# The second attention's pooling branch: values copied and exponentials scaled by another engine, a bias folded once

## What is computed

```python
q = jnp.broadcast_to(slot_query, (Bx, NS, D))            # 16 slots
o = q + _mha(q, x, x, d_Wq, d_bq, d_Wk, d_bk, d_Wv, d_bv, d_Wo, d_bo)
# _mha: scores = (q Wq + bq)(x Wk + bk) / 4 ; attn = softmax(scores)
#       out = (attn (x Wv + bv)) Wo + bo
# then: 16 experts, one per slot, work on o; a last attention reads o from every token
```

## Time and profile before

| | |
|---|---|
| median of 3 runs | 1344.31 us (1343.42 to 1347.88) |
| profiled execution | 1347.85 us, span 1346.1 us |
| mean granted TensorE clock | 0.984 of 2.4 GHz |
| TensorE busy | 1280.9 us, 95% of the span |
| VectorE busy | 927.0 us, 69% |
| ScalarE busy | 805.5 us, 60% |
| POOL busy | 747.9 us, 56% |
| chain that ended last | TensorE 86%, VectorE 5%, DMA 3%, ScalarE 2% |

### The profile page before, as it was taken

How to read it: one execution, slowest core, us unless ns; L and a number is a source line. 1 busy time by engine, 2 the same in 40 slices (tenths; PEclk the granted TensorE clock), 3 DMA queues, 4 the chain that set the end, 5 groups by cost and what they waited for, 6 DMA issues and landing times.

```text
span 1346.1 us, 38344 instructions
## 1 busy us (share of the span) xinstructions
PE 1280.9 (95%) x14758; PEld 1143.9 (85%) x14758; DVE 927.0 (69%) x2426; ACT 805.5 (60%) x1794; POOL 747.9 (56%) x836
## 2 busy tenths in 40 slices
PE   7999999997999999999999988999999998899898
PEld 6888888886899999999999977899999997555476
DVE  3899999997576566555555027999999997221386
ACT  3676776663666777777676435666666665332453
POOL 1377777765478777777876034566666643100231
PEclk8999999998999999999999989999999999999999
DMA  5665554543667676777766811631111110599811
GB/s 173 214 223 192 189 168 165 190 166 108 231 214 217 223 223 220 226 232 228 218 220 224 327 44 29 236 116 49 49 49 56 56 32 29 215 430 429 322 64 64
DMA packets 103892, 237.52 MB, mean 176 GB/s; under 512 B 8992, under 2 KB 86176, under 8 KB 91296
## 3 DMA queue, kind: packets, MB, share of 16 engines
q1 hardware_dynamic: 97568, 218.29, 47.1%
q0 software_dynamic: 6144, 16.79, 3.9%
HBM read 174.22 MB, written 60.82 MB: 175 GB/s over the span
## 4 chain that ended last, share of the span: by engine, by line
PE 86%; DVE 5%; DMA 3%; ACT 2%; issue 2%; SPq 0%; POOL 0%; DVEq 0%; ACTq 0%; PEldq 0%; POOLq 0%
PE ps L1640 13%; PE psT L1625 6%; PE ps L648 6%; PE psS L625 5%; PE ps L802 5%; PE ps L852 5%; PE psT L634 4%; PE ps L661 4%; PE psS L1625 3%; PE ps L1625 3%; PE ps L785 2%; PE ps L815 2%; PE ps L742 2%; PE psT L640 2%; PE ps L1878 2%
## 5 line engine op out<-in xcount | busy, mean ns | idle before, releaser
L1593 POOL TENSOR_TENSOR wb_lo<-arena,wb_hi 128x2048 fp32r<-128x2048 f32 x64 | 298.0, 4657 | 96.7 <-ACT wb_hi L1713 96.7
L1640 PE MATMUL ps<-wb_hi,hT_hi 128*128 128x256 f32 x528 | 152.0, 288 | 2.5 <-DVE hT_lo L1766 2.5
L634 PE MATMUL psT<-arena 32*128 32x128 f32 x2048 | 151.2, 286 | 0.4 <-ACT arena L955 0.4
L1640 PE MATMUL ps<-wb_lo,hT_hi 128*128 128x256 f32 x528 | 149.3, 283 | 0.0
L1640 PE MATMUL ps<-wb_hi,hT_lo 128*128 128x256 f32 x528 | 148.4, 281 | 0.0
L625 PE MATMUL psS<-arena 32*128 32x256 f32 x1024 | 142.8, 397 | 1.2 <-ACT arena L955 0.5
L1713 ACT CAST wb_hi<-arena 128x1024 fp32r<-128x1024 f32 x128 | 130.6, 1045 | 11.3 <-DMA arena<-w_dram 10.7
L634 PEld LDWEIGHTS psT<-arena 32*128 32x128 f32 x2048 | 126.5, 189 | 1.1 <-issue 0.6
L1236 POOL TENSOR_TENSOR arena<-arena,eps_sb 128x1 f32<-128x1 f32 x96 | 23.8, 248 | 164.7 <-DVE arena L1113 114.2
L1778 DVE TENSOR_TENSOR arena<-ps,arena 128x512 f32<-128x512 f32 (+1 forms) x39 | 25.4, 650 | 117.4 <-PE ps L1640 77.0
L625 PEld LDWEIGHTS psS<-arena 32*128 32x128 f32 x1024 | 95.2, 191 | 9.9 <-issue 6.7
(11 more groups left out here) (400 smaller groups left out, 3920.5 us busy)
## 6 DMA issues: line engine op xcount, KB each, us to landing
arena<-wset_dram SPq DMA_DIRECT2D x24, 2048.0 KB, 14.5
xs_rows<-arena SPq DMA_DIRECT2D x33, 1024.0 KB, 5.0
arena<-w_dram SPq DMA_DIRECT2D x32, 1028.0 KB, 6.0
arena<-w_dram SPq DMA_DIRECT2D x32, 1024.0 KB, 5.9
arena<-w_dram SPq DMA_DIRECT2D x7, 2052.0 KB, 13.5
w_sb<-xs_rows SPq DMA_DIRECT2D x33, 256.0 KB, 2.7
xs_rows<-arena SPq DMA_DIRECT2D x33, 256.0 KB, 5.6
arena<-ctxT_dram SPq DMA_DIRECT2D x63, 128.0 KB, 2.3
```

The costliest lines, as they stand in the source:

```text
L634: nc.tensor.matmul(psT[:, b, j * P:(j + 1) * P], kbd[p, (k - 1) % 3, c, par, :], qT[p, (k - 1) % 3, c, :], start=j == 0, stop=False, skip_ ...
L1593: nc.gpsimd.tensor_tensor(wb_lo[:, u % 2, part], wb_raw[:, u % 2, part], wb_hi[:, u % 2, part], ALU.subtract).then_inc(w_g.sem, 1)
L1640: last = nc.tensor.matmul(ps[5][:, t * D:(t + 1) * D], hp[:, f, t * P:(t + 1) * P], wp[:, f, :], start=f == 0 and t == 0 and n == 0, stop= ...
```

## The change

The values' bias leaves the loop. Ahead of the steps TensorE multiplies `dbv` (now a column, spread over 128 columns as the stationary operand) with the output weights `do` into ps[4], and VectorE adds this to the row `dbo` before its first step; TensorE's step 0 waits for that. In the loop ScalarE copies the values without bias, one step later than VectorE did (for k-5, behind the copy L952 and ahead of the exponentials L955), and scales the exponentials by the reciprocals in two instructions, behind a wait for the reciprocals. VectorE loses the addition L1213, the product L1088 and the negation L1173: the queries and their bias are folded with a minus sign, so that L1170 takes a minimum, which is the negated maximum, and L1037 applies a scale of -1.

```diff
...
 WEIGHTS = ["q0", "k0", "v0", "o0", "q1", "k1", "v1", "o1", "dv", "do", "cq", "ck", "cv", "co"]
-ROWS = ["bo0", "dbv", "dbo", "cbo"]
-COLS = ["bq0", "bk0", "bv0", "dbq", "dbk", "cbq", "cbk", "cbv", "gamma", "beta", "bo0"]
+ROWS = ["bo0", "dbo", "cbo"]
+COLS = ["bq0", "bk0", "bv0", "dbq", "dbk", "cbq", "cbk", "cbv", "gamma", "beta", "bo0", "dbv"]

...
         mk = carve(C, HC, NS)
-        smx = carve(2)
-        snx = carve(2)
+        smn = carve(2)
         sz = carve(2)
...
             for n, name in ((1, "dbq"), (2, "cbq")):
-                nc.vector.tensor_scalar(qcol[:, n, :], col[name], QSCALE, None, ALU.mult)
+                nc.vector.tensor_scalar(qcol[:, n, :], col[name], -QSCALE if n == 1 else QSCALE, None, ALU.mult)
             for c in range(C):
...
                 x1_p = track(n + "x1_p", "xT s V")
-                x1_a = track(n + "x1_a", "xT e0 e1")
-                x1_v = track(n + "x1_v", "s0 s1 neg V")
+                x1_a = track(n + "x1_a", "xT e0 e1 V")
+                x1_v = track(n + "x1_v", "s0 s1")
                 x2_p = track(n + "x2_p", "pT av")
-                x2_a = track(n + "x2_a", "pT")
-                x2_v = track(n + "x2_v", "rz pn mask sum")
+                x2_a = track(n + "x2_a", "pn pT")
+                x2_v = track(n + "x2_v", "rz mask sum")
                 st_x = [sem(n + "st_x0"), sem(n + "st_x1")]
...
                     else:
-                        before(pe, x1_v.sem, x1_v.at(i - 6, "V"))
+                        before(pe, x1_a.sem, x1_a.at(i - 6, "V"))
                         before(pe, x2_v.sem, x2_v.at(i - 7, "mask"))
...
                         last.then_inc(stash_p, 1)
+                    for c in range(C):
+                        last = nc.tensor.matmul(ps[4][:, 0:D], col["dbv"][:, c:c + 1].to_broadcast([P, P]), w["do"][:, c, :],
+                                                start=c == 0, stop=c == C - 1)
+                    last.then_inc(setup_p, 1)
                 for k in steps:
...
                         pe.wait_ge(stash_a, STASH + LATE)
+                        pe.wait_ge(setup_v, 8)
                     if not A and k == B + 4:
...
                     if not A and valid(k - 5):
-                        pe.wait_ge(x2_v.sem, x2_v.at(k - 5, "pn"))
+                        pe.wait_ge(x2_a.sem, x2_a.at(k - 5, "pn"))
                         before(pe, pre_a.sem, pre_a.at(k + 1, "xT"))
...
                         pe.wait_ge(x2_a.sem, x2_a.at(k - 5, "pT"))
-                        pe.wait_ge(x1_v.sem, x1_v.at(k - 5, "V"))
+                        pe.wait_ge(x1_a.sem, x1_a.at(k - 5, "V"))
                         for m in range(C):
...
                         nc.scalar.copy(avS.rearrange("p g t -> p (g t)"), ps[4][:, :]).then_inc(av_a.sem, 1)
+                    if not A and valid(k - 5):
+                        act.wait_ge(x1_p.sem, x1_p.at(k - 5, "V"))
+                        before(act, x2_v.sem, x2_v.at(k - 6, "mask"))
+                        nc.scalar.copy(dVb[:, (k - 5) % 2, :], ps[5][:, D:2 * D]).then_inc(x1_a.sem, 1)
+                        act.wait_ge(x2_v.sem, x2_v.at(k - 5, "rz"))
+                        before(act, x2_p.sem, x2_p.at(k - 6, "pT"))
+                        for c in range(C):
+                            last = nc.scalar.activation(pn[:, c, :], sc[:, c, :], ACT.Identity, bias=0.0, scale=srz[:, c:c + 1])
+                        last.then_inc(x2_a.sem, 1)
                     if valid(k - 1):
...
                     if not A and valid(k - 4):
-                        act.wait_ge(x1_v.sem, x1_v.at(k - 4, "neg"))
-                        before(act, x2_v.sem, x2_v.at(k - 5, "pn"))
+                        act.wait_ge(x1_v.sem, x1_v.at(k - 4, "s1"))
                         for c in range(C):
-                            nc.scalar.activation(sc[:, c, :], sc[:, c, :], ACT.Exp, bias=snx[:, c:c + 1],
+                            nc.scalar.activation(sc[:, c, :], sc[:, c, :], ACT.Exp, bias=smn[:, c:c + 1], scale=-1.0,
                                                  accum_out=sz[:, c:c + 1]).then_inc(x1_a.sem, 1)
...
                     dve.wait_ge(a0_last["res"].sem, a0_last["res"].at(B - 1, "res"))
+                    dve.wait_ge(setup_p, 2)
+                    nc.vector.tensor_tensor(row["dbo"], ps[4][:, 0:D], row["dbo"], ALU.add).then_inc(setup_v, 1)
                 for k in steps:
...
                         nc.vector.reciprocal(srz, sz).then_inc(x2_v.sem, 1)
-                        dve.wait_ge(x2_v.sem, x2_v.at(sl_i, "rz"))
-                        before(dve, x2_p.sem, x2_p.at(sl_i - 1, "pT"))
-                        nc.vector.tensor_tensor(pn, sc, srz[:, :, None].to_broadcast([P, C, P]), ALU.mult)\
-                            .then_inc(x2_v.sem, 1)
                     if valid(cur):
...
                         dve.wait_ge(x1_p.sem, x1_p.at(rt_i, "s"))
-                        before(dve, x2_v.sem, x2_v.at(sl_i, "pn"))
+                        before(dve, x2_a.sem, x2_a.at(sl_i, "pn"))
                         for c in range(C):
                             nc.vector.tensor_scalar(sc[:, c, :], ps[4][:, c * P:(c + 1) * P], qac[:, c:c + 1], None,
-                                                    ALU.add, ALU.max, accum_out=smx[:, c:c + 1]).then_inc(x1_v.sem, 1)
-                        dve.wait_ge(x1_v.sem, x1_v.at(rt_i, "s1"))
-                        nc.vector.tensor_scalar(snx, smx, -1.0, None, ALU.mult).then_inc(x1_v.sem, 1)
+                                                    ALU.add, ALU.min, accum_out=smn[:, c:c + 1]).then_inc(x1_v.sem, 1)
                     if valid(nxt):
...
                                                 ALU.mult).then_inc(x2_v.sem, 1)
-                    if not A and valid(rt_i):
-                        dve.wait_ge(x1_p.sem, x1_p.at(rt_i, "V"))
-                        before(dve, x2_p.sem, x2_p.at(rt_i - 1, "av"))
-                        nc.vector.tensor_tensor(dVb[:, rt_i % 2, :], ps[5][:, D:2 * D], row["dbv"], ALU.add)\
-                            .then_inc(x1_v.sem, 1)
                     if not A and valid(sl_i):
...
                         for m in range(C):
-                            nc.vector.tensor_scalar(sqT[:, m, :], ps[7][:, m * NS:(m + 1) * NS], QSCALE, qcol[:, 1, m:m + 1],
+                            nc.vector.tensor_scalar(sqT[:, m, :], ps[7][:, m * NS:(m + 1) * NS], -QSCALE, qcol[:, 1, m:m + 1],
                                                     ALU.mult, ALU.add).then_inc(prep_v, 1)
...
                f[p + "d_Wv"], f[p + "d_Wo"], f[p + "c_Wq"], f[p + "c_Wk"], f[p + "c_Wv"], f[p + "c_Wo"]]
-    rows = [f["L0_xattn_b_o"], f[p + "d_bv"], f[p + "d_bo"], f[p + "c_bo"]]
+    rows = [f["L0_xattn_b_o"], f[p + "d_bo"], f[p + "c_bo"]]
     cols = [f["L0_xattn_b_q"], f["L0_xattn_b_k"], f["L0_xattn_b_v"][heads], f[p + "d_bq"], f[p + "d_bk"], f[p + "c_bq"], f[p + "c_bk"], f[p + "c_bv"],
-            f["L0_ffn_gamma"], f["L0_ffn_beta"], f["L0_xattn_b_o"]]
+            f["L0_ffn_gamma"], f["L0_ffn_beta"], f["L0_xattn_b_o"], f[p + "d_bv"]]
     t = np.arange(P)
...
```

## The result

| | before | after |
|---|---|---|
| median, 11 runs each | 1348.79 us (1342.83 to 1351.28) | 1356.96 us (1351.95 to 1367.01) |
| ratio after to before, 95% interval | | 1.0074 (1.0050 to 1.0098) |
| profiled execution, span | 1347.85, 1346.1 us | 1357.45, 1355.7 us |
| mean granted TensorE clock, profiled | 0.984 | 0.976 |
| TensorE busy, share of the chain | 1280.9 us, 86% | 1290.0 us, 84% |

The change is slower by 0.74%, more than the 0.3% that can be told from nothing, and 1356.96 us is above the range. The ratios, and the differences of means further down, leave out every run that lies over 1.5% above the fastest run of the same kernel: two of the kernel before (1360.67 and 1361.92 us) and two of the twelve of the kernel with the later addition (1363.52 and 1364.07 us; with them its difference of means would be +3.4 ± 4.1 and not +0.7 ± 2.3).

A forecast was written before the change was run, and what follows sets the result against it. The prediction took TensorE to bound the kernel. It summed 2.8 (wait), 0.6 (clock) and 0.2 (tail) to +3.6 us, added to the median 1344.31: 1347.9 us, range 1344.5 to 1351.2.

The forecast's parts named there:

- the term for the clock: Start of second attention: L701 and L802 may run at the lower clock after the wait; +0.6 us, bounds 0 and 1.2.
- VectorE relieved, worth 0: Steps: about 1.0 us less VectorE work per block gains 0, as TensorE covers it or scores release the chain.
- B: Stash steps: VectorE had paced them, so four TensorE waits of 0.78 us go; 1344.8 us, chance 0.13.
- C: All 26 steps: VectorE had paced them, hidden in TensorE's record; 26 x 1.0 us less, 1321.9 us, chance 0.07.
- ScalarE's new work, worth 0 in the steps: Steps: value copy and two scalings, 1.1 us per block, delay L955 up to 0.35 us, still covered; cost 0.
- Rival D: All 26 steps: ScalarE becomes late at exponentials L955; +13 us at 0.5 us over, 1360.9 us, chance 0.08.
- The wait, +2.8: Ahead of the first step: VectorE waits for TensorE's product, L1108 starts 2.9 us late; +2.8 us, bounds 2.4 and 3.0.
- rival A: Start of second attention: the lower clock lasts longer, the full level needing the next dense stretch; +6.6 us, 1350.9, chance 0.12.
- The tail, +0.2: Last steps: ScalarE's copy L976 stands behind scalings that wait for the reciprocal; +0.2 us, bounds -0.7 and +1.1.

The follow-up runs named there:

- wait only: Kernel before plus only the product, VectorE's wait, an addition into an unread row and TensorE's wait for it: 1353.35 us, ratio 1.0037.
- addition later: Changed kernel with VectorE's wait and bias addition moved to the start of step 0, TensorE's wait for it to step 1: 1347.43 us, ratio 1.0011.
- the tail reordered: ScalarE's scalings for the last three blocks moved behind the copy into x_all: 1351.25 us on the changed kernel, 1345.35 us on addition later.

## Why the prediction was wrong

It gave 1347.9 us, a range up to 1351.2, and 0.55 for no change; 1356.96 came. The miss of 9.1 us has two halves.

**The base, 4.5 us.** I added to 1344.31, the median of the three runs shown. The same kernel's median was 1348.79 over eleven runs, 1345.7 to 1348.0 in the next three groups and 1343.1 in the last; over all 112 runs it is 1347.0, so some 2.7 us of the 4.5 are the base and the rest is where this group of eleven happened to lie. And the profiled execution (1347.85) was nearer to most of these medians than 1344.31 was. "Its steps being regular" was no ground to put its 3.5 us extra aside: it had 44 us at the lower level, which is the usual amount.

**The change, 8.2 us by the medians in place of 3.6.** The step that failed is the term for the clock: +0.6 us behind the wait, with 1.2 as its upper bound, and nothing at all in the tail. Point by point:

- *VectorE relieved, worth 0: right.* The 0.43 us from TensorE's last pair of scores to L1093, alike in a stash step and a late one, decided it: the waits at L772 did not shrink, and VectorE's time became idle time ahead of L1103. Rivals B and C are refuted by the rows above.
- *ScalarE's new work, worth 0 in the steps: right.* The pair of scalings was put at 0.70 and takes 0.70. The exponentials start no later than before and TensorE does not wait: 232.88 of 233 us. Rival D is refuted. The Trainium skill, "ScalarE: Activation LUTs", Rules for kernel authors, which wants multiplications on VectorE, holds here for the price of the operation (0.70 against 0.43) and has no bearing on the time of the steps, since neither engine is the one that ends them.
- *The wait, +2.8: right.* 2.93 in the profile, at the place and by the chain described, and 9.54 to 9.56 in every kernel that has it.
- *The clock behind it, +0.6, bounds 0 and 1.2: wrong.* I priced only two groups of products that would run at the lower level, as if its length stayed. The profiled execution shows 4.17 - 2.93 = 1.2 by the stage's last block. On the mean it is more: the wait cost 5.8 ± 3.1 (wait only against before), 7.7 ± 3.2 (changed kernel against addition later) and 5.5 ± 3.8 (the same with the tail reordered), on average 6.3 ± 1.9, so some 3.4 ± 1.9 beyond the direct 2.9. The profiled executions agree: the last block's row maxima are at 340.0 us from the clearing of m2 on the mean of the five with the wait and no spare products, and at 335.4 in the four without the wait, 4.6 later. This is rival A, to which I gave 0.12. Its 6.6 us hold 6.4 for the wait with its clock, close to the 6.3 measured; its chance was too low. Its picture, that the full level misses one dense stretch and needs the next, was not tested. The Trainium skill, "TensorE: Matmul & The Clock Gate", Part 1, says that activity lifts the clock and idleness brings it back down; the profiles here agree (0.50 from 803.1 us on, 1.8 us after the end of the idle 3.62 in the changed kernel; in three of the other four with this wait and no spare products the level was down already when the wait ended, in the fourth 0.9 us behind it; 1.00 up to about 800 us with spare products in it), and I had the rule in hand and weighed it too lightly.
- *The tail, +0.2: right at the full level, and wrong in what it left out.* From the slot scores at 1146.21 the steps are 6.04, 5.47 and, at the full level, 3.12 us, against 5.27, 6.06 and 3.12 before: +0.18. But the same reordering leaves TensorE idle for 1.97 us twice instead of 1.2, and the lower level comes into the tail more often and for longer: 1.3 us in the profiled execution. The profiled tails with the changed kernel's order take 2.3 us more on the mean than those with the order of before. By the means of runs the rest of the change costs 2.6 ± 3.9 (changed kernel against wait only) or 0.7 ± 2.3 (addition later against before), so its size is open and no cost at all is not excluded. I had written that the tail has no cover, and did not ask what its clock would do.

Summed up: 6.3 ± 1.9 for the wait and some 2 for the tail make about 8; measured are +9.3 and +8.4. That the wait with its clock is the larger part is shown; how the rest is shared is not. How much of that is a single execution's chance is seen in the kernel before: its 112 runs go from 1337.5 to 1361.9 us, and within the runs of a kernel the time rises by 0.3 to 0.6 us for each us at the lower level. What decides in a given run how soon the full level returns stays open; no run here was made to settle it.

## What to carry to other kernels

Where one engine has no idle time for hundreds of us, relieving another is worth nothing, and the test is a row: does the relieved engine's work end before, or with, what releases the chain? A wait set ahead of a pipeline's first step costs its length and then what the clock does: look at how thin TensorE's work becomes around it, at the start and in the tail, and put a one-time operation where its input has long been there; here one line moved by two steps took back the wait. And take the base from as many runs as the forecast's precision needs: a third of a per cent cannot be counted from three.

## What was not expected of the hardware

Spare products on TensorE, read by no one, filled an idle wait; the clock kept its full level 4 to 8 us longer behind it, and the first row maxima came 1.3 to 2.3 us earlier (16.74 and 16.81 against 18.03 to 19.05); for the whole kernel the means are 2.8 ± 4.5 and, with the tail reordered, 1.1 ± 4.2 lower, which is not clear of nothing. Twice as many held the real work up by 3.1 us. Nine spread over the thin steps, and three that fitted their gaps, brought the time at the lower level from 37 to 29 and 32 us a run, and the time by nothing that can be measured. And the order of ScalarE's work, which moved no more than 0.9 us of the chain, went with whether TensorE's clock fell in the tail: it did in six of six profiled executions with the changed kernel's order, in two of three with the order of before, and in none of five with the scalings behind the copy.
